# Moving the attention sum and its moments into the recurrence, and joining three stages of a transformer-like layer into one

## The chip, the cores and the metric

The kernel runs on one core of a Trainium2 chip. The core has a matrix engine (PE in the profile, with its weight loads as PEld), a vector engine (DVE), a scalar engine (ACT), a general engine (POOL) and a synchronising engine (SP) that only issues DMAs here. The metric is the device time of one launch in microseconds; lower is better. A profile comes from one execution, and its times are counted from the start of its span.

## The reference, cut to what matters

The input x has 4 sequences (B) of 1,024 rows (T) of 256 numbers (D). Four sublayers follow one another, each adding to x:

```
x = x + recurrence(layernorm(x), ctx)       # scan over 1024 steps
x = x + ffn(layernorm(x))                   # int8 weights, int16 activations
x = x + cross_attention(layernorm(x), ctx)  # 16 heads, 64 context rows
x = x + mixture_of_experts(layernorm(x))    # 8 experts, switch routing

def step(carry, x_t):                       # inside recurrence
    h0, c0, h1, c1, a = carry
    xin = concatenate([x_t, a])
    h0, c0 = lstm_cell(xin, h0, c0, ...)
    h1, c1 = lstm_cell(h0, h1, c1, ...)
    q = h1 @ Wq.T
    attn = softmax(einsum('bh,bsh->bs', q, context))
    a2 = tanh(concatenate([einsum('bs,bsh->bh', attn, context), h1]) @ Wo.T + bo)
    return (h0, c0, h1, c1, a2), a2

def quantize_a16(x):                        # before each of the ffn's two products
    amax = clip(max(abs(x)), 1e-8)          # over the whole tensor
    scale = 32767.0 / amax
    return clip(round(x * scale)) / scale
```

What the recurrence returns at step t is one row of 256 numbers for each of the 4 sequences, and it is needed by step t + 1. The maximum in `quantize_a16` is over the whole tensor, so the ffn's first product can't start before every row is normalised, and its second not before every hidden value is known.

## The kernel before

x lies in the core's own memory as `xres`: 8 groups (NB) of 128 rows for each of the 4 sequences, so 32 tiles of 128 x 256 (NT = 32). The program is a row of stages with a barrier between them, each stage giving every engine its own straight list of instructions and loops. Order is set by that list and by semaphores: an engine waits until a count is reached, and no planner reorders anything.

`front` loads and prepares. `scan` runs the 1,024 steps. PE, ACT and DVE each hold a loop of two steps a turn; on DVE the first 28 steps are written out one by one, since 25 of them carry a piece of other work in the *gaps*: `step(t, s, between)` calls `between(0)` after the first layer's new state, `between(1)` after the second layer's, and `between(2)` after the turned attention sum. In these gaps the ffn's weights are searched for their maximum (128 x 256 at a time, line 431), scaled and rounded. The result of a step is written to `a_hist[:, t, k, b]` by line 496: 128 partitions hold the feature, steps run along the free axis, the eight (k, b) pairs lie interleaved. POOL does nothing in this stage, and SP only loads.

`add_attention_and_normalize` (called the add stage below) then brings a_hist into xres. For each of 32 tiles POOL copies two strided 128 x 128 pieces out of a_hist (line 538), PE turns them, DVE adds them (line 585), takes the row's moments (lines 78 and 81), gets the standard deviation from ACT, normalises (line 89) and searches the tile's largest value (line 599).

`ffn_hidden` makes the 1,024 hidden values of all rows. `ffn_output` multiplies them: DVE quantises a 128 x 1,024 tile in two passes (lines 759 and 762), PE multiplies it in 8 matmuls (line 742; the hardware profile counts each in two records, since they are float32), POOL adds the output's bias to x beforehand, and DVE adds the product (line 768, `finish`). `release_semaphores` clears every semaphore used so far, one instruction each on SP, while all other engines wait at the barrier. `prepare_attention` loads the cross-attention's weights and masks (lines 822 to 827), makes keys and values of the 64 context rows, and `queries` normalises each tile of x, turns it (line 912) and multiplies it (line 922) into the queries of four tiles at a time. Here `in_steps` staggers parts of the work over tiles: `in_steps(eng, [(a, 0), (b, 1)], ...)` runs a on tile t and then b on tile t - 1. Then `attention`, routing and the experts follow, and nothing is changed in their work.

## Time and profile before

| | us |
|---|---|
| three runs | 8344.06, 8344.10, 8343.58 (median 8344.06) |
| the profiled execution | 8346.82 |
| its span in the trace | 8345.0 |

| stage | from | to | length |
|---|---|---|---|
| front | 0 | 54.1 | 54 |
| scan | 54.1 | 7279.9 | 7226 |
| add_attention_and_normalize | 7280.5 | 7353.0 | 72.6 |
| ffn_hidden | 7353.0 | 7451.3 | 98.2 |
| ffn_output | 7451.3 | 7567.9 | 116.6 |
| release_semaphores | 7567.9 | 7574.4 | 6.5 |
| prepare_attention | 7574.4 | 7601.0 | 26.6 |
| queries | 7601.0 | 7676.8 | 75.8 |
| attention | 7676.8 | 7873 | 196 |
| routing, scattering, experts | 7873 | 8345 | 472 |

The stages were read off the timeline: each begins where its first instruction starts. In the rows further down, "busy" is the time in which an engine had an instruction running, `x` is the number of records, and the bracket at the end of a timeline row says how long the engine stood idle just before it and which instruction ended that. PEclk is the share of full speed that the throttle granted PE: 0.50 is 1.2 GHz, 1.00 is 2.4 GHz.

### The profile page before, as it was taken

What the parts mean: (1) busy time and instruction counts of PE and PEld (TensorE: products, weight loads), DVE (VectorE), ACT (ScalarE), POOL (GpSimd) and SP (SyncE); (2) the same over time, 40 slices, a digit from 0 to 9 for tenths busy, and PEclk for the clock granted to TensorE, in tenths of its full rate; (3) what the DMA queues carried; (4) which work ended last, traced back from release to release, by engine and by line L of the source; (5) the groups of instructions that cost most, each with busy time, mean ns of one, the idle gap of its engine ahead of it and who ended that gap; (6) DMA issues with size and microseconds to landing.
All of it is one profiled execution on the core that took longest, in us unless ns stands there. A gap on an engine that the chain in (4) does not pass through costs nothing. (4 is left out here: it accounts for less than half of the span.)

```text
span 8345.0 us, 815594 instructions
## 1 busy us (share of the span) xinstructions
PE 6831.2 (82%) x380504; PEld 5806.1 (70%) x380505; DVE 4214.3 (51%) x21197; ACT 3382.3 (41%) x17078; POOL 332.6 (4%) x342
## 2 busy tenths in 40 slices
PE   7888888888888888888888888888888888766769
PEld 5777777777777777777777777777777777644546
DVE  5555454455454454554544544454454544575822
ACT  4444444444444444444444444444444444432422
POOL 0000000000000000000000000000000000021622
PEclk8999999999999999999999999999999999988879
DMA  2000000000000000000000000000000000000143
GB/s 86 5 0 0 0 0 0 0 0 0 0 0 0 0 0 0 0 0 0 0 0 0 0 0 0 0 0 0 0 0 0 0 0 0 0 6 18 65 165 107
DMA packets 58666, 94.52 MB, mean 11 GB/s; under 512 B 14202, under 2 KB 45952, under 8 KB 57472
## 3 DMA queue, kind: packets, MB, share of 16 engines
q1 hardware_dynamic: 53248, 81.38, 3.0%
q0 software_dynamic: 5376, 12.63, 0.4%
q8 instruction: 20, 0.33, 0.0%
q14 instruction: 22, 0.18, 0.0%
HBM read 76.08 MB, written 20.00 MB: 12 GB/s over the span
## 5 line engine op out<-in xcount | busy, mean ns | idle before, releaser
L307 PE MATMUL scan_sums<-rec_wh,scan_hT 128*4 128x64 f32 x131008 | 2394.2, 219 | 2.6 <-issue 2.5
L428 DVE STREAM_TRANSPOSE scan_sums<-scan_sums 128x64 f32<-128x64 f32 x6144 | 1546.6, 266 | 1137.2 <-PE scan_sums L307 1136.7
L307 PEld LDWEIGHTS scan_sums<-rec_wh,scan_hT 128*4 128x4 f32 x131008 | 1991.4, 89 | 3.4 <-issue 3.4
L307 PE MATMUL scan_sums<-rec_wa,scan_aT 128*4 128x64 f32 (+1 forms) x65536 | 1104.7, 219 | 381.8 <-ACT scan_aT L389 381.8
L307 PEld LDWEIGHTS scan_sums<-rec_wa,scan_aT 128*4 128x4 f32 (+1 forms) x65536 | 915.6, 88 | 570.6 <-ACT scan_aT L389 570.6
L307 PE MATMUL scan_sums<-rec_wx,scan_xT 128*4 128x64 f32 (+1 forms) x65536 | 1291.6, 219 | 7.4 <-issue 6.5
L307 PE MATMUL scan_sums<-rec_wi,scan_hT 128*4 128x64 f32 (+1 forms) x65536 | 1103.1, 219 | 142.5 <-issue 2.5
L307 PEld LDWEIGHTS scan_sums<-rec_wi,scan_hT 128*4 128x4 f32 (+1 forms) x65536 | 914.3, 88 | 331.1 <-DVE scan_hT L478 328.5
L307 PEld LDWEIGHTS scan_sums<-rec_wx,scan_xT 128*4 128x4 f32 (+1 forms) x65536 | 1023.7, 89 | 8.1 <-issue 7.1
L373 ACT ACTIVATE scan_tanh_f<-scan_sums 128x8 f32<-128x8 f32 x2048 | 364.0, 178 | 1188.0 <-DVE scan_sums L428 1188.0
L368 ACT ACTIVATE scan_sums<-rec_bias 128x192 f32<-128x192 f32 x2050 | 686.8, 335 | 302.8 <-PE scan_sums L347 5.5
L389 ACT ACTIVATE scan_aT<-scan_a_sum 128x8 f32<-128x8 f32 x1024 | 182.0, 178 | 1517.8 <-DVE scan_a_sum L493 1517.8
L317 PE MATMUL scan_scores<-rec_kp,scan_hT 128*4 128x64 f32 x16384 | 416.6, 219 | 369.3 <-DVE scan_hT L478 369.3
L317 PE MATMUL scan_a_sum<-rec_vp,scan_pT 128*4 128x64 f32 x16384 | 416.9, 219 | 299.3 <-DVE scan_pT L490 299.3
L375 ACT ACTIVATE scan_scanned<-scan_sums 128x16 f32<-128x16 f32 x2048 | 394.7, 193 | 541.8 <-DVE scan_sums L428 541.8
L317 PEld LDWEIGHTS scan_scores<-rec_kp,scan_hT 128*4 128x4 f32 x16384 | 227.7, 85 | 554.6 <-DVE scan_hT L478 554.6
L478 DVE SCALAR_TENSOR_TENSOR scan_hT<-scan_tanh_o,scan_sums 128x8 f32<-128x8 f32 x2048 | 335.2, 164 | 466.5 <-ACT scan_sums L380 466.5
L317 PEld LDWEIGHTS scan_a_sum<-rec_vp,scan_pT 128*4 128x4 f32 x16384 | 228.0, 86 | 484.6 <-DVE scan_pT L490 484.6
L493 DVE STREAM_TRANSPOSE scan_a_sum<-scan_a_sum 128x64 f32<-128x64 f32 x1024 | 272.2, 266 | 547.7 <-PE scan_a_sum L317 547.7
L482 DVE TENSOR_REDUCE scan_neg_max<-scan_scores 128x1 f32<-128x65 f32 x1024 | 231.4, 226 | 536.1 <-PE scan_scores L317 536.1
L384 ACT ACTIVATE scan_exps<-scan_scores,scan_neg_max 128x65 f32<-128x65 f32 x1024 | 324.9, 317 | 432.1 <-DVE scan_neg_max L482 432.1
L476 DVE TENSOR_TENSOR_SCAN scan_sums<-scan_scanned 128x24 f32<-128x24 f32 x2048 | 443.8, 217 | 71.7
(254 smaller groups left out, 6166.6 us busy)
## 6 DMA issues: line engine op xcount, KB each, us to landing
experts_bias<-in_b SPq DMA_DIRECT2D x40, 640.0 KB, 4.4
moe_w<-in_w SPq DMA_DIRECT2D x16, 1024.0 KB, 12.3
slots_x<-route_blank SPq DMA_DIRECT2D x40, 129.0 KB, 2.5
experts_x<-slots_x SPq DMA_DIRECT2D x40, 129.0 KB
w_xres<-in_x_steps SPq DMA_DIRECT2D x8, 512.0 KB, 11.1
w_xres<-in_x SPq DMA_DIRECT2D x4, 1024.0 KB
x_rows<-w_xres SPq DMA_DIRECT2D x4, 1024.0 KB, 11.3
rec_wh<-in_wh SPq DMA_DIRECT2D x2, 1024.0 KB, 14.8
```

The lines of the kernel that those rows point to most:

```text
L307: last = nc.tensor.matmul(sums[layer][BANK[g]][32 * j:32 * j + ROWS[g], 0:64], state[:, k, FIRST[g]:FIRST[g] + ROWS[g]], weight[:, k, j, 6 ...
L317: last = nc.tensor.matmul(bank[32 * j:32 * j + B, 0:64], state[:, k, :], weight[:, k, j, :], start=start and k == 0, stop=stop and k == 1, ...
L368: nc.scalar.activation(layer_sums[l][:, :, 0:64], w["bias"][:, l, :, :], ACT.Copy).then_inc(seeded[l], 1)
L373: nc.scalar.activation(tanh_f[l][:], gates_of[l][F][:, :, 0:B], ACT.Tanh).then_inc(f_tanh[l], 1)
L375: nc.scalar.activation(ig_terms[l], gates_of[l][IG][:, :, 0:2 * B].rearrange("p k (f b) -> p k f b", f=2), ACT.Tanh).then_inc(c_terms[l], 1)
L384: nc.scalar.activation(exps[:], scores[:, 0:S + 1], ACT.Exp, bias=neg_max[:], accum_out=total).then_inc(exps_done, 1)
L389: nc.scalar.activation(state_of(aT), a_sumT.rearrange("p (k u) -> p k u", k=2)[:, :, 0:B], ACT.Tanh).then_inc(a_ready, 1)
L428: nc.vector.transpose(turned[l][g], sums[l][g][:, 0:64]).then_inc(gates_turned[l][g], 1)
L476: nc.vector.tensor_tensor_scan(cell[l], flat[l][:, 0], flat[l][:, 1], 0.0, ALU.mult, ALU.add).then_inc(c_done[l], 1)
L478: nc.vector.scalar_tensor_tensor(state_of(hT[l]), tanh_o[l][:], 1.0, tanh_c[l].rearrange("p (k b) -> p k b", k=2), ALU.add, ALU.mult).then ...
L482: nc.vector.tensor_reduce(neg_max[:], scores[:, 0:S + 1], AX.X, ALU.max, negate=True).then_inc(max_done, 1)
L493: nc.vector.transpose(a_sumT, a_sum[:, 0:64]).then_inc(a_turned, 1)
```

## The change

It has three parts.

First, in `scan`: when the 128 steps of a group are over, POOL copies their eight (b, k) pieces out of `a_hist` into `part`. In the first four steps of the next group DVE turns them in gaps 0 and 1, one piece a gap (`turn_part`), with its own transposes, which act within blocks of 32 x 32. SP writes them to `a_rows` in DRAM with 32 DMAs so that rows come out in order, and reads the four tiles back into `mid` with one DMA. In steps 7 and 8 of the group DVE adds them to xres (`fold`), in 9 and 10 it takes the row statistics (`spread`), in 11 and 12 it aggregates them, and in 13 it keeps the moments. This is done for groups 1 to 7, so for 28 of the 32 tiles; the last four tiles have no later steps. DVE's loop of steps therefore becomes eight loops, with 14 steps written out ahead of seven of them. PE's and ACT's lists in the scan stay.

Second, `add_attention_and_normalize` adds only the four last tiles, from PE's transposes of a_hist itself. ACT takes one square root for 28 tiles and one for 4, and does the normalising, which DVE did; DVE makes the factors and searches the 32 maxima.

Third, `ffn_output`, `prepare_attention` and `queries` become one stage, `output_and_queries`. In one staggered loop a tile is quantised, multiplied, finished, normalised, turned and projected; keys and values are made at its end. The loads are issued at the start of the stage, and PE and DVE wait for all nine of them (`ALL_LOADS`) before their first tile; the eight loads of masks are issued once the last tile is quantised. Buffers are cut out of `hidden` and `ffn_xn` (class `Arena`). The clearing of semaphores, 128 of them where it was 102, comes after this stage.

The diff, cut to its core:

```diff
+            @block.gpsimd
+            def _(pool):
+                nc.gpsimd.sem_inc(staged, 2 * B)
+                with pool.Fori(1, NB) as g:
+                    for b in range(B):
+                        for k in range(2):
+                            pool.wait_ge(a_kept, g * P)
+                            pool.wait_ge(staged, 2 * B * g)
+                            nc.gpsimd.tensor_copy(part[:, b, k, :], a_hist[:, bass.ds(g * P - P, P), k, b]).then_inc(part_done, 1)
...
+                for g in range(1, NB):
+                    sp.wait_ge(staged, 2 * B * g + 2 * B)
+                    for b in range(B):
+                        rows = a_rows[b, bass.ds(g * P - P, P), :].rearrange("(q r) (j k u) -> j r k q u", q=4, j=4, k=2)
+                        for j in range(4):
+                            for k in range(2):
+                                sp.dma_start(rows[j][:, k], stage[32 * j:32 * j + 32, b, k, :].rearrange("p (q u) -> p q u", q=4)).then_inc(rows_out, 16)
+                    sp.wait_ge(rows_out, ROWS_OUT * g + ROWS_OUT)
+                    sp.wait_ge(folded, B * g)
+                    sp.dma_start(mid[:], a_rows[:, bass.ds(g * P - P, P), :].rearrange("b p d -> p b d")).then_inc(mid_in, 16)
...
+                def turn_part(g, b, k):
+                    dve.wait_ge(part_done, 2 * B * g)
+                    dve.wait_ge(rows_out, ROWS_OUT * g)
+                    nc.vector.transpose(stage[:, b, k, :], part[:, b, k, :]).then_inc(staged, 1)
+
+                def fold(g, b):
+                    x = tile_of(xres, g - 1, b)
+                    dve.wait_ge(mid_in, 16 * g)
+                    nc.vector.tensor_tensor(x, mid[:, b, :], x, ALU.add).then_inc(folded, 1)
...
+                def late(g, at):
+                    def between(gap):
+                        if gap == 2:
+                            return
+                        if at < 4:
+                            turn_part(g, at, gap)
+                        elif 7 <= at < 9:
+                            fold(g, 2 * (at - 7) + gap)
+                        elif 9 <= at < 11:
+                            spread(g, 2 * (at - 9) + gap)
+                        elif 11 <= at < 13:
+                            gather_moments(g, 2 * (at - 11) + gap)
+                        elif at == 13 and gap == 0:
+                            keep_moments(g)
+                    return between
 
...
-                with dve.Fori((PLAIN + 3 * FC + 1) // U, T // U) as i:
+                with dve.Fori((PLAIN + 3 * FC + 1) // U, P // U) as i:
                     t = i * U
                     for s in range(U):
                         step(t, s)
+                dve.wait_ge(ffn["x_in"], 16 * (B + 1))
+                LATE = 14
+                for g in range(1, NB):
+                    for at in range(LATE):
+                        step(g * P + at, 0, late(g, at))
+                    with dve.Fori((g * P + LATE) // U, (g + 1) * P // U) as i:
+                        t = i * U
+                        for s in range(U):
+                            step(t, s)
                 dve.wait_ge(a_kept, T)
+                dve.wait_ge(moments_kept, NB - 1)
...
-                nc.tensor.sem_inc(sum_done, 2)
+                for b in range(B):
+                    for k in range(2):
+                        last = nc.tensor.transpose(turned[b][:, P * k:P * k + P], a_hist[:, P * LAST:P * NB, k, b], w["ident"][:])
+                    last.then_inc(turned_done, 1)
...
+                def normalize(n):
+                    g, b = n // B, n % B
+                    nc.scalar.activation(xn[:, g, b, :], xres[:, g, b, :], ACT.Identity, bias=shift[:, g, b:b + 1],
+                                         scale=rstd[:, g, b:b + 1]).then_inc(xn_done, 1)
+                act.wait_ge(eps_done, 1)
+                deviations(0)
+                for f in range(2):
+                    keep_weight(f)
+                act.wait_ge(shift_done, 1)
+                for n in range(B * LAST):
+                    normalize(n)
+                    if n == 2 * B:
+                        act.wait_ge(moments_done, B)
+                        deviations(1)
+                    if n % B == B - 1 and 2 + n // B < FC:
+                        keep_weight(2 + n // B)
+                act.wait_ge(shift_done, 2)
+                for n in range(B * LAST, NT):
+                    normalize(n)
...
-                in_steps(dve, [(add, 0), (moments, 0), (normalize, 1), (largest, 2)])
+                add(0)
+                factors(0)
+                for b in range(1, B):
+                    add(b)
+                for b in range(B):
+                    spread(b)
+                for b in range(B):
+                    gather_moments(b)
+                for n in range(2 * B + 1):
+                    largest(n)
+                factors(1)
+                for n in range(2 * B + 1, NT):
+                    largest(n)
...
-                in_steps(pe, [(turn, 0), (project, 1)], NB // 2, 2 * B)
...
+                in_steps(pe, [(produce, 1), (turn, 5), (project, 6)], NB // 2, 2 * B)
...
-                in_steps(act, [(deviation, 0), (keep, 1), (keep_queries, 3)], NB // 2, 2 * B)
...
+                in_steps(act, [(deviation, 2), (keep, 5), (keep_queries, 7)], NB // 2, 2 * B)
...
-                in_steps(dve, [(moments, 0), (normalize, 1)])
...
+                dve.wait_ge(loaded, ALL_LOADS)
+                nc.vector.tensor_scalar(h["bq"][:], h["bq"][:], DH ** -0.5, None, ALU.mult).then_inc(built, 1)
+                in_steps(dve, [(finish, 2), (quantize, 0), (moments, 2), (normalize, 3)], NB // 2, 2 * B)
...
+        ALL_LOADS = 16 * (len(loads) + 2)
...
                 for b in range(B):
-                    sp.dma_start(mask_int[:, :, b, :], ins["mask"][b].rearrange("(g p) s -> p g s", p=P)).then_inc(loaded, 16)
-                    sp.dma_start(w["group_prob"][:, :, b, :], ins["fside"][b].rearrange("(g p) s -> p g s", p=P)).then_inc(loaded, 16)
+                    sp.dma_start(mask_int[:, :, b, :], ins["mask"][b].rearrange("(g p) s -> p g s", p=P)).then_inc(masks_in, 16)
+                    sp.dma_start(h["group_prob"][:, :, b, :], ins["fside"][b].rearrange("(g p) s -> p g s", p=P)).then_inc(masks_in, 16)
```

Two helpers of the merged stage, `produce` on PE and `finish` on DVE, wait as follows:

```diff
+                pe.wait_ge(w["out_in"], 32)
+                pe.wait_ge(loaded, ALL_LOADS)
+
+                def produce(i, t):
+                    n = number(i, t)
+                    pe.wait_ge(hq_done, n)
+                    pe.wait_ge(out_done, n)
+                    for f in range(FC):
+                        last = nc.tensor.matmul(summed[t % 2][:, 0:D], hq[t % 2][:, f, :], w["w_out"][:, f, :], start=f == 0, stop=f == FC - 1)
+                    last.then_inc(sum_done, 1)
 
...
+                def finish(i, t):
+                    n = number(i, t)
+                    x = tile_of(xres, *tile(i, t))
+                    dve.wait_ge(bias_done, n)
+                    dve.wait_ge(sum_done, n)
+                    nc.vector.scalar_tensor_tensor(x, summed[t % 2][:, 0:D], back[:], x, ALU.mult, ALU.add).then_inc(out_done, 1)
+
+                def moments(i, t):
+                    dve.wait_ge(out_done, number(i, t) + 2)
+                    norm_moments(nc, dve, norm, number(i, t), t % 2, tile_of(xres, *tile(i, t)))
+
+                def normalize(i, t):
+                    n = number(i, t)
                     dve.wait_ge(turned_done, n)
-                    norm_apply(nc, dve, norm, n, b % 2, tile_of(xres, g, b), xn[b % 2][:]).then_inc(xn_done, 1)
```

### How the order of instructions moves

In the scan DVE's instructions of a looped step stood like this (the first layer's gates, its state `scan_hT`, then the second layer's gates):

```order
L472 SCALAR_TENSOR_TENSOR scan_scanned<-scan_tanh_f,scan_c 128x8 [waits scan_f_tanh0]
L428 STREAM_TRANSPOSE scan_sums<-scan_sums 128x64 [waits scan_summed_o0]
L475 REGISTER_ALU
L476 SCALAR_TENSOR_TENSOR scan_sums<-scan_scanned 128x24 [waits scan_c_terms0]
L478 SCALAR_TENSOR_TENSOR scan_hT<-scan_tanh_o,scan_sums 128x2x4 [waits scan_h_factors0]
L428 STREAM_TRANSPOSE scan_sums<-scan_sums 128x64 [waits scan_summed_f1]
L428 STREAM_TRANSPOSE scan_sums<-scan_sums 128x64 [waits scan_summed_ig1]
```

In the changed program the first written-out step of a group has a turned piece between the two layers, and one behind the second:

```order
L561 SCALAR_TENSOR_TENSOR scan_scanned<-scan_tanh_f,scan_c 128x8 [waits scan_f_tanh0]
L476 STREAM_TRANSPOSE scan_sums<-scan_sums 128x64 [waits scan_summed_o0]
L565 SCALAR_TENSOR_TENSOR scan_sums<-scan_scanned 128x24 [waits scan_c_terms0]
L567 SCALAR_TENSOR_TENSOR scan_hT<-scan_tanh_o,scan_sums 128x2x4 [waits scan_h_factors0]
L517 STREAM_TRANSPOSE scan_stage<-scan_part 128x128 [waits scan_rows_out,scan_part_done]
L476 STREAM_TRANSPOSE scan_sums<-scan_sums 128x64 [waits scan_summed_f1]
```

The second layer's first transpose now stands behind one that waits for POOL's eight copies (`scan_part_done`).

POOL, which had no instruction in the scan, has this at the head of its new loop there, eight copies a turn:

```order
L318 UNCONDITIONAL_BRANCH
L318 ISA
L322 REGISTER_ALU [waits scan_a_kept]
L323 ISA [waits scan_staged]
L323 COPY scan_part<-a_hist 128x128
L323 ISA [waits scan_staged,scan_a_kept]
```

So the first copy is released by the last write of the group (`scan_a_kept`), the next ones follow one another.

On PE, the loop of `ffn_output` had one tile's eight matmuls after another, and behind its end came a barrier and the wait for all loads of `prepare_attention`:

```order
L742 MATMUL output_summed<-ffn_xn 128x256 [waits output_out_done,output_hq_done]
L742 MATMUL output_summed<-ffn_xn 128x256 x7
L736 REGISTER_ALU
L736 COMPARE_AND_BRANCH
L731 UNCONDITIONAL_BRANCH
L842 UNCONDITIONAL_BRANCH [waits barrier_Pool_Activation_PE_DVE_SP_release]
L847 MATMUL heads_k_sum<-heads_ctxT,heads_wk 128x256 [waits heads_loaded]
L847 MATMUL heads_k_sum<-heads_ctxT,heads_wk 128x256 x3
```

In the merged stage a tile's two transposes and every fourth time the queries' four matmuls stand between them:

```order
L942 MATMUL output_summed<-ffn_xn 128x256 [waits output_out_done,output_hq_done]
L942 MATMUL output_summed<-ffn_xn 128x256 x7
L950 MATMUL output_turned<-w_ident,output_xn 128x128 [waits output_xT_done,output_xn_done]
L950 MATMUL output_turned<-w_ident,output_xn 128x128
L956 REGISTER_ALU
L958 ISA [waits output_xT_done]
L960 MATMUL output_q_sum<-ffn_xn 128x512 [waits output_q_done]
L960 MATMUL output_q_sum<-ffn_xn 128x512
L958 REGISTER_ALU
L960 MATMUL output_q_sum<-ffn_xn 128x512 [waits output_q_done]
L960 MATMUL output_q_sum<-ffn_xn 128x512
L939 REGISTER_ALU
```

The transposes and projections of queries, which had a stage of their own, now share PE's list with the ffn's second product.

## Rows read from the trace of the kernel before

**Rows 1.** Busy by stretch: length, PE, PEld, DVE, ACT, POOL (records), PEclk, DMA, GB/s.
```profile
54.00:7280.00 7226.00, 6019.81 (x376780) 5269.86 (x376780) 3617.38 (x19538) 3026.31 (x16387) 0.00 (x0) 1.00 0.00 1
7280.00:7353.00 73.00, 25.09 (x80) 11.96 (x80) 59.41 (x290) 22.78 (x48) 28.06 (x65) 0.50 0.00 0
...
7451.00:7568.00 117.00, 113.50 (x512) 99.10 (x512) 64.98 (x100) 0.00 (x0) 29.09 (x32) 0.97 0.00 0
...
7601.00:7677.00 76.00, 48.93 (x128) 22.24 (x128) 33.64 (x193) 28.44 (x82) 0.26 (x1) 0.84 0.00 0
```

**Rows 2.** Timeline of DVE in a looped step: start, length, instruction, [idle before, releaser].
```profile
7254.75 0.17 DVE L496 TENSOR_SCALAR a_hist<-scan_aT 128x8 f32 x1 [0.35 <-ACT scan_aT L389]
...
7256.55 0.16 DVE L478 SCALAR_TENSOR_TENSOR scan_hT<-scan_tanh_o,scan_sums 128x8 f32<-128x8 f32 x1 [0.23 <-ACT scan_sums L380]
7257.24 0.27 DVE L428 STREAM_TRANSPOSE scan_sums<-scan_sums 128x64 f32<-128x64 f32 x1 [0.53 <-PE scan_sums L307]
```

**Rows 3.** Timeline of DVE, gap 1 of a written-out step with a maximum in it.
```profile
98.11 0.41 DVE L431 TENSOR_REDUCE scan_amax<-ffn_raw 128x1 f32<-128x256 f32 x1
98.72 0.23 DVE L482 TENSOR_REDUCE scan_neg_max<-scan_scores 128x1 f32<-128x65 f32 x1 [0.20 <-PE scan_scores L317]
```

**Rows 4.** POOL's strided copies of the add stage: minimum/median/maximum ns, first and last start.
```profile
L538 POOL COPY first_part<-a_hist x64: 403/410/571, 7280.8 to 7342.3; 128x128 f32 x64
```

**Rows 5.** DVE's SBUF transposes of the scan: busy us, mean ns | idle before.
```profile
L486 DVE STREAM_TRANSPOSE scan_expsT<-scan_exps 128x64 f32<-128x64 f32 x1024 | 230.8, 225 | 0.0
L488 DVE STREAM_TRANSPOSE scan_invT<-scan_inv 128x32 f32<-128x32 f32 x1024 | 184.3, 180 | 0.0
```

**Rows 6.** SP: first and last of nine load issues, the last's landing, and the clears.
```profile
7574.45 0.34 SPq L822 DMA_DIRECT2D heads_ctxT<-in_ctxT  x1
...
7578.15 0.43 SPq L824 DMA_DIRECT2D heads_bo_heads<-in_bo_k  x1
...
DMA to landing us min/median/max: 4.3/4.3/4.3
...
L40 SPq EVENT_SEMAPHORE_RANGE_CLEAR  x102: 25/30/49, 7567.9 to 7574.2; - x102
```

**Rows 7.** Timelines of DVE and ACT: last maxima of the add stage; two 128x256 passes.
```profile
7351.05 0.74 DVE L599 TENSOR_REDUCE first_row_max<-ffn_xn 128x1 f32<-128x256 f32 x2
...
7676.78 0.72 ACT L1038 ACTIVATE attn_q<-heads_q_all 128x256 f32<-128x256 f32 x2 [0.42 <-ACTq L1032]
```

**Rows 8.** Timeline of PE: 67 records of the product, a tile's transposes, a projection.
```profile
7488.72 14.62 PE L742 MATMUL output_summed<-ffn_xn 128*128 128x256 f32 x67
...
7645.19 0.44 PE L912 MATMUL query_turned<-w_ident,query_xn 128*128 128x128 f32 x2 [0.64 <-DVE query_xn L89]
7645.47 3.61 PE L922 MATMUL query_summed<-query_xT,heads_wq 128*128 128x512 f32 x8
```

**Rows 9.** Timeline of DVE in ffn_output: finish, and the quantising's second pass.
```profile
7494.70 0.48 DVE L768 SCALAR_TENSOR_TENSOR w_xres<-output_summed,output_back,w_xres 128x256 f32 x1 [1.58 <-PE output_summed L742]
...
7495.88 0.69 DVE L762 TENSOR_SCALAR ffn_xn<-ffn_xn 128x1024 f32<-128x1024 f32 x1
```

**Rows 10.** Timeline of DVE in prepare_attention.
```profile
7590.02 0.90 DVE L868 COPY heads_twice<-heads_ctxT 128x256 f32<-128x256 f32 x4 [22.42 <-DMA heads_group_prob<-in_fside]
7590.84 1.22 DVE L870 TENSOR_SCALAR heads_neg<-heads_mask_int 128x2048 f32<-128x2048 int32 x1
...
7592.74 4.91 DVE L876 TENSOR_TENSOR heads_keys<-heads_kT,heads_head_mask 128x512 f32<-128x512 f32 x8 [0.60 <-ACT heads_kT L861]
...
7599.01 1.43 DVE L884 TENSOR_TENSOR heads_values<-heads_v,heads_pair_mask 128x256 f32<-128x256 f32 x4
```

**Rows 11.** DMA: instruction fetches in 54 to 285, none in 7300 to 7352, 7259 to 7280.
```profile
q14 instruction: 5, 0.04, 0.1%
...
DMA packets 0, 0.00 MB, mean 0 GB/s; under 512 B 0, under 2 KB 0, under 8 KB 0
...
q8 instruction: 5, 0.08, 1.6%
```

382 lines of the change are left out of this document (182 added, 200 removed).

## The prediction

> **What bounds the kernel now.** I read the table of stretches first [rows 1]. It shows that 7,226 of 8,345 us are the recurrence, where no engine is full: PE is busy 6,020 us and DVE 3,617. A step depends on the one before, so what counts there is a chain through PE, DVE and ACT, 7,226 / 1,024 = 7.06 us a step, and idle time between its links is free for other work. The reader should then look at the add stage: 73 us, DVE busy 59.4, PE at its lower clock and nearly idle. DVE bounds it. In the ffn's output PE is busy 113.5 of 117 us and bounds it. In the queries nothing is full (PE 48.9, DVE 33.6 of 76), and between the two lie 33 us of clearing and loading in which hardly anything computes.
>
> The timeline of a step comes second [rows 2]: DVE writes a_hist at 7254.75 to 7254.92, has the first layer's state at 7256.71 and is idle until the second layer's sums reach it at 7257.24. That 0.53 us is gap 0.
>
> **Scan: what is added.** A group's first gap 0 holds a transpose that waits for eight POOL copies. The copies can start when a_hist is written; I allow 0.3 us for the semaphore and POOL's registers. A copy of this shape took 0.41 us [rows 4], eight take 3.3, so they end at 7254.92 + 0.3 + 3.3 = 7258.5 in the times of [rows 2]. The transpose of 128 columns is not in the trace: 64 took 0.225 and 32 took 0.180 us [rows 5], 0.045 for each further 32, so I take 0.18 + 3 x 0.045 = 0.315, of which some 0.08 overlaps the next instruction (DVE's neighbours start before the one ahead has ended). The second layer's first transpose, due at 7257.24, then starts at about 7258.8: 1.55 us late, with PE, ACT and the rest of the chain waiting behind it. Seven groups: 7 x 1.55 = 10.9 us. With the shortest copy, 0.403, and no allowance it is 8; with the longest, 0.571, (8 x 0.571 = 4.6) it is 7 x 2.85 = 20.
>
> The other inserts I cost at nothing. A 0.41 us maximum in gap 1 still left 0.20 us idle in front of the next reduction [rows 3], so a gap swallows about 0.6 us. The additions of 128 x 256 and the statistics should take 0.4 to 0.5 us (the same width as the maximum), the other transposes 0.32, the aggregations less. If one of the 12 longer inserts of a group spilled over by 0.1 us, that would be 7 x 12 x 0.1 = 8 us, which I keep in the range.
>
> The data must come back before gap 0 of the group's eighth step. The last transpose is issued in gap 1 of the fourth step, about 4.2 us after that step's start, gap 0 lies at 1.8: 4 x 7.06 + 1.8 - 4.2 = 25.8 us. SP issues one DMA every 0.46 us (nine issues, 7574.45 to 7578.15 [rows 6]), so 32 take 14.8 us; a landing took 4.3, and the load back another 0.5 + 4.3. Together 23.9 us: in time by 2 us. DVE also leaves a loop and enters straight code seven times; its step periods before and after its one loop entry in the trace are alike, and I take nothing. Scan: **+11**, from +8 to +28.
>
> **Add stage: what is removed.** DVE's 59.41 us over 32 tiles are 1.86 a tile [rows 1], two of its passes over 128 x 256 being 0.37 each (0.74 for a pair [rows 7]). What stays for the last four tiles is 4 x (1.86 - 0.74) = 4.5 us. Then come 32 maxima; two stand in 0.74 us with 0.41 for one, so they follow each other every 0.33: 10.6 us. The normalising moves to ACT, where two passes of that width took 0.72 us [rows 7], 0.31 to 0.36 each. ACT starts some 4 us before DVE's maxima and has 32 of these and eight copies of turned weights, 40 x 0.36 = 14.4, so it stays just ahead or costs up to 3 us. Lead 1.3 (PE's first transposes at the low clock), roots and factors 0.7, tail to the next stage 1.2 (7351.79, where the last maximum ended, to 7353.0). Sum: 1.3 + 4.5 + 0.7 + 10.6 + 1.2 = 18.3 us where it was 72.6: **-54**, from -50 to -57.
>
> **The merged stage.** Before, output to the start of attention took 7676.8 - 7451.3 = 225.5 us. Now:
> Start: nine loads, 3.7 us of issues and 4.3 to land [rows 6], then one scaling and the first tile's quantising, 1.4 [rows 9], and hand-overs: PE starts at +9.9. This is new: the load's latency is no longer behind anything, and everything behind the wait on PE and DVE stands still.
> Loop: PE has per tile 16 records of 14.62 / 67 = 0.218 us, 3.49, two transposes that hold it for 7645.47 - 7645.19 = 0.28 us, and every fourth tile a projection of 3.5 [rows 8]. Until the last product that makes 32 x 3.49 + 27 x 0.28 + 6 x 3.5 = 140.3, plus 3 for the clock's start (it is at its lower level while PE idles for the loads; before, the output stage lost 113.5 - 111.7 = 1.8 [rows 1]). DVE has per tile finish and quantising, 7494.70 to 7496.57 = 1.87 us [rows 9], and norm work of 33.64 / 32 = 1.05 [rows 1]: 2.9, less than PE's 3.5 to 4.6. So PE bounds it, and the last product ends at +153.2.
> End: finish, moments, root, normalising, transposes, a copy, the last projection and the key product follow one another: 0.5 + 1.1 + 0.3 + 0.3 + 0.4 + 3.6 + 1.8 and 3.5 of hand-overs = 11.5. Behind them DVE's keys 4.9, masks 1.2, values in two steps of 1.4 [rows 10] = 8.9. So +173.6. The mask loads (11.4 us from 7578.6 to 7590.0, where they released DVE [rows 6, 10]) start before the last product and hide behind this.
> Clearing: 102 clears took 6.3 us, 0.062 each [rows 6]; 128 take 7.9, with the barrier 8.6.
> Sum 182.2 against 225.5: **-43**. If PE stayed at 1.2 GHz in the first tiles longer, or hand-overs cost more, -36; if the tail overlaps better, -47.
>
> **Sum.** +10.9 - 54.3 - 43.3 = -86.7. The span of 8345.0 becomes 8258.3. The profiled run took 8346.82, the median of the runs 2.8 less; 8344.06 - 86.7 = 8257.4, and I take **8258 us**. Its own terms range from about 8246 to 8275.
>
> **Rivals.** (a) *The rows come back late.* The 32 stores scatter 128 bytes at a time, which no transfer of the trace does, so their time may be longer than 4.3 us. Every microsecond over the 2 in hand costs 7 us. With 5 us more: 7 x 3 = +21, 8279; this lies against nothing in the profile but the small margin. (b) *The merged loop is bound by a chain, not by PE.* DVE's list puts finish, quantising and normalising in one order, and PE's transposes wait for DVE in the middle of products. If PE waits once a tile for the norm work of 1.05 us, 32 x 1.1 = +35, 8293. For it speaks that DVE's 2.9 us and PE's 3.8 leave under 1 us; against it that transposes lie five steps behind. (c) *The merging overlaps nothing,* so that the joined stage takes its old 225 us: 8301. The order of rows on PE speaks against it, and only a semaphore's count that lags could do it. (d) *Slower: code is fetched again in each turn of a loop.* DVE's list in the scan grows from about 1,500 to 3,900 instructions. In the straight-line start, five pages of 8 KB were fetched for DVE in 231 us, and PE at the end of the scan needed five of 16 KB in 21 us, so up to 3.6 us for one after another is the price [rows 11]. By the program's listing three of the eight DVE loops lie across a boundary of 128 instructions, 57 turns each, 171 turns. If each turn had to fetch both pages again at 3.6 us a turn, this adds 171 x 3.6 = 616, less 87: 8873 us. It decides the sign from 87 / 171 = 0.5 us a turn. Against it: the DVE loop of the add stage lies across such a boundary as well, and between 7300 and 7352 not one packet of code was moved [rows 11].
> The Trainium skill, page "Runtime: NRT & Kernel Launch", section "Instruction fetch mechanics", says that a taken branch forces a fetch if its target isn't in the present window of two pages. By that rule a loop across one boundary stays inside the window and costs nothing, and the trace agrees, with 0 packets in the add stage's loop.
>
> On the copies, the profile shows them slower beside a busy DVE (0.571 at most against 0.403 [rows 4]). The Trainium skill, page "SBUF — State Buffer", has DVE and GpSimd share a port pair as an exclusive lock, held for a whole instruction. By it a copy would wait for a DVE instruction that reads twice from SBUF, and each of the few such in the 3.3 us would add its 0.2 us once a group, 7 x 0.6 = 4 us on the sum above.
>
> **Chances.** The forecast with its own range 0.74; (a) 0.10; (b) 0.06; (c) 0.02; (d) 0.03; something else, spread between 8275 and 8340, 0.05. To hold 8 in 10 the range takes the forecast's terms and most of (a): **8246 to 8288**. A measurement can tell a difference of about 0.2%, 17 us, from none. All but (d) and a little of the last lie below 8327: faster 0.96, same 0.01, slower 0.03.
>
> **What the changed profile would show.** The steps should have a period of about 7.05 us everywhere but in the first step of seven groups, where it should be near 8.6, with DVE idle on POOL's copy. Steps 7 to 13 of a group with longer periods would show spilled inserts, a wait of DVE on the load into `scan_mid` at step 7 would show (a). The add stage should last 18 us with DVE's maxima in a row. The merged stage should begin with 8 us of waiting for loads; then PE should be over 90% busy at 2.4 GHz, with DVE's `finish` released by PE. PE idle on `xn` or `hq` would show (b). Instruction packets in the loops would show (d). The prediction fails if the scan's period in the loops moves at all: 0.02 us there is 18 us.

## The result and the profile after

The changed kernel took 8255.51 us (median of four runs, 8253.7 to 8255.79); the kernel before took 8344.08 on the same chip. The ratio is 0.9892, with a 95% interval of 0.9881 to 0.9904: 88.6 us less, where 86 had been forecast. The profiled execution took 8255.78 us, its span is 8254.0, against 8345.0 before: 91.0 less.

Where the 91 us came from, stage by stage, each counted from its first instruction to the next stage's:

| stretch | before | after | change | forecast |
|---|---|---|---|---|
| front | 54.1 | 55.1 | +1.0 | 0 |
| scan, first instruction to last | 7225.8 | 7230.9 | +5.1 | +10.9 |
| last step to ffn_hidden | 73.1 | 22.9 | -50.2 | -54.3 |
| ffn_hidden | 98.2 | 99.1 | +0.9 | 0 |
| output to attention | 225.5 | 179.5 | -46.0 | -43.3 |
| attention to the end | 668.2 | 666.4 | -1.8 | 0 |

The table of stretches of the changed kernel shows it (length, PE, PEld, DVE, ACT, POOL with records, PEclk, DMA share, GB/s). It answers [rows 1]:

```profile
55.00:7286.30 7231.30, 6016.91 (x376780) 5266.86 (x376780) 3655.59 (x19741) 3026.63 (x16387) 20.62 (x56) 1.00 0.01 2
7286.30:7309.00 22.70, 6.27 (x24) 3.98 (x24) 17.12 (x55) 19.88 (x43) 0.38 (x1) 0.59 0.00 1
...
7408.00:7418.00 10.00, 0.03 (x1) 0.06 (x1) 2.83 (x9) 0.00 (x0) 1.62 (x2) 0.59 0.54 158
7418.00:7430.00 12.00, 12.00 (x44) 10.12 (x45) 6.75 (x12) 1.58 (x2) 11.61 (x15) 0.78 0.01 1
7430.00:7560.00 130.00, 129.69 (x579) 103.90 (x578) 87.23 (x272) 26.14 (x70) 16.84 (x23) 1.00 0.06 10
7560.00:7579.00 19.00, 12.28 (x44) 7.46 (x42) 10.67 (x26) 4.98 (x11) 0.00 (x0) 0.95 0.25 45
7579.00:7587.50 8.50, 0.00 (x0) 0.00 (x0) 0.00 (x0) 0.00 (x0) 0.00 (x0) 0.50 0.00 1
```

The reader should see three things. In the scan DVE is busy 38 us longer than before, and the scan is only 5 us longer: most of the moved work stands in time that was idle. In the short add stage ACT is busier (19.9 of 22.7) than DVE (17.1), which the prediction didn't have. And in the merged stage PE is busy 129.7 of 130 us at full clock, behind 10 us in which it does nothing and 12 at the lower level or mixed.

The timeline of DVE in the first step of a group shows the one place where the scan pays:

```profile
974.52 0.17 DVE L585 TENSOR_SCALAR a_hist<-scan_aT 128x8 f32 x1 [0.35 <-ACT scan_aT L435]
...
976.44 0.16 DVE L567 SCALAR_TENSOR_TENSOR scan_hT<-scan_tanh_o,scan_sums 128x8 f32<-128x8 f32 x1 [0.23 <-ACT scan_sums L426]
977.97 0.31 DVE L517 STREAM_TRANSPOSE scan_stage<-scan_part 128x128 f32<-128x128 f32 x1 [1.37 <-POOL scan_part L323]
978.21 0.35 DVE L476 STREAM_TRANSPOSE scan_sums<-scan_sums 128x64 f32<-128x64 f32 x2
...
979.33 0.16 DVE L567 SCALAR_TENSOR_TENSOR scan_hT<-scan_tanh_o,scan_sums 128x8 f32<-128x8 f32 x1 [0.23 <-ACT scan_sums L426]
```

And POOL's own timeline there, eight copies in one row:

```profile
974.99 2.95 POOL L323 COPY scan_part<-a_hist 128x128 f32 x8 [972.09 <-DVE a_hist L585]
```

DVE waits 1.37 us for POOL. The copies run from 974.99 to 977.94, so one follows another every 0.36 us, though each is recorded with 0.42. The second layer's first transpose starts 3.69 us after the write of a_hist began, where it was 2.49 in [rows 2]: 1.20 late. But the steps are only 0.76 us longer (7.79 for 7.03 in six groups, 7.82 in the one shown). While DVE waited, PE had finished all of the second layer's sums, so the transposes that before waited for them one by one (0.53 and 0.18 idle) now follow at once: from the first of them to the new state it takes 1.12 us instead of 1.42, and another 0.12 comes back at the step's end.

The trace shows a second thing in this step. While POOL copies, the two instructions with which DVE updates the first layer's cell take longer:

```profile
975.52 0.28 DVE L561 SCALAR_TENSOR_TENSOR scan_scanned<-scan_tanh_f,scan_c 128x8 f32<-128x8 f32 x1
...
975.89 0.32 DVE L565 TENSOR_TENSOR_SCAN scan_sums<-scan_scanned 128x24 f32<-128x24 f32 x1
```

In the first step of the seven groups they have 0.24 to 0.28 and 0.30 to 0.32 us, in all other steps at most 0.17 and 0.22, and the first layer's state is about 0.1 us late. It costs nothing here, since DVE then waits for POOL in any case.

### The profile page after: what moved, and what is told of

Same layout as the page of the kernel before. It is cut to its first block and busy times, and to the rows that moved or that the text cites. A ratio compares the mean times of both kernels' runs of the same rounds, so it can differ in the third digit from the quotient of the medians.

```text
span 8254.0 us, 814880 instructions
## 1 busy us (share of the span) xinstructions
PE 6793.0 (82%) x380441; PEld 5788.2 (70%) x380449; DVE 4208.6 (51%) x21164; ACT 3382.8 (41%) x17073; POOL 313.9 (4%) x334
```

## Experiments

Medians of one table aren't from one chip, so each is given with the kernel before beside it. Between the traces of kernels whose looped steps are the same, the mean period of such a step varied from 7.029 to 7.039 us, which is up to 10 us over the scan; for a few microseconds I therefore go by the length of the stage in question in the traces, and by the medians only for the whole.

### The parts alone

One kernel has the scan and the add stage of before and the merged stage of the change; the other the reverse (both are the two programs' functions put together, nothing else is edited).

> The recurrence and the add stage as before, and only the third part of the change: output, preparation and queries as one stage. If the parts are independent, as the comparison of the two traces has it (merged stage 179.5 us where the three stages and the clearing had 225.5), the median is 8344 - 46 = 8298 us, and the scan's period stays at 7.03 us. Rival: the merged stage owes part of its gain to the shorter scan code or the buffers left by the other parts; then its length is not 179.5 but nearer 190.

> The first two parts of the change alone: additions and moments in the recurrence's gaps, and the short add stage; output, preparation and queries as before. By the traces: scan +5.1, add stage 22.4 instead of 72.6, so 8344 + 5 - 50 = 8299 us. The sum of this gain and that of the merging alone should be 90 within 2 us. Rival: the two parts share a gain (for one, fewer stages); then the sum differs by more.

Merging alone: 8298.65 us against 8341.59, 42.9 less (ratio 0.9947, 0.9931 to 0.9964). In its trace the stage up to attention lasts from 7448.1 to 7627.3, 179.1 us. Scan and add stage alone: 8300.24 against 8341.59, 41.4 less (0.9948, 0.9931 to 0.9965); scan 7228.4, add stage 21.9 us, seven steps with a period of 7.77 to 7.81. The two sum to 84.3, not to the 90 within 2 that I expected, and both together gave 88.6; but the interval of each is some 14 us wide either way, so the medians can't tell. The stages' lengths can: they are the same alone and together, but for the scan's 7228.4 against 7230.9, which is the period of the looped steps (7.030 against 7.033). So there is no sign that the parts share a gain, and the merging needs nothing from the rest.

### The wait for POOL in the first gap

```diff
-                        if at < 4:
-                            turn_part(g, at, gap)
-                        elif 7 <= at < 9:
-                            fold(g, 2 * (at - 7) + gap)
...
+                        n = 2 * at + gap
+                        if 1 <= n < 9:
+                            turn_part(g, (n - 1) // 2, (n - 1) % 2)
+                        elif 15 <= n < 19:
+                            fold(g, n - 15)
```

> The changed kernel with every insert of a group one gap later: the first turned piece stands in gap 1 of the group's first step, so that POOL's eight copies have 4 us and not 1.8 before DVE asks for them. My theory: the only cost of the inserts is the wait for POOL in the first gap 0, 0.76 us a group in the trace. It should vanish: every period 7.03, the scan 7 x 0.76 = 5.3 us shorter, 8250 us. Rival: the wait moves to gap 1 or the extra 128x128 transpose in a gap costs by itself; then periods of 7.3 or more stay in the first step, or a later step pays because the rows come back too late (the return has now 0.7 us in hand where it had 5.6).

8247.34 us against 8341.59: 94.3 less (0.9886, 0.9869 to 0.9902). The medians' intervals overlap with the changed kernel's, so the trace decides. In it no step of a group's start is longer any more; of 1,023 periods only the first two, the last two and the eight at which DVE enters a loop stand out. The same transpose, in gap 1:

```profile
979.23 0.16 DVE L568 SCALAR_TENSOR_TENSOR scan_hT<-scan_tanh_o,scan_sums 128x8 f32<-128x8 f32 x1 [0.23 <-ACT scan_sums L426]
979.31 0.31 DVE L517 STREAM_TRANSPOSE scan_stage<-scan_part 128x128 f32<-128x128 f32 x1
979.92 0.22 DVE L572 TENSOR_REDUCE scan_neg_max<-scan_scores 128x1 f32<-128x65 f32 x1 [0.30 <-PE scan_scores L363]
```

It starts at once, and the reduction behind it comes 0.69 us after the state began, as it always does: the insert itself costs nothing. So the wait for POOL was the whole price of the inserts, 7 x 0.76 = 5.3 us. POOL's copies still lengthen DVE's two instructions in the first step (0.23 to 0.28 and 0.30 to 0.32 us), and with no wait behind them the step's period is 6.99 to 7.04, so that is absorbed too. The eight loop entries cost 0.11 us each, seven more than before: 0.8 us, which I had put at nothing.

### How much a gap holds

Both row statistics of steps 9 and 10 in one gap:

```diff
-                            spread(g, 2 * (at - 9) + gap)
+                            if gap == 0:
+                                spread(g, 2 * (at - 9))
+                                spread(g, 2 * (at - 9) + 1, False)
```

> The changed kernel with both row statistics of steps 9 and 10 of a group in gap 0 of the step, one behind the other, and gap 1 left empty. The prediction held that a gap of 0.53 us swallows about 0.6 us of work. Two statistics keep DVE for 0.42 + 0.35 = 0.77 us and should make these two steps 0.1 to 0.2 us longer each (7.15 to 7.25). Rival: a link behind absorbs it, as 0.4 of the 1.2 us of the wait for POOL were absorbed; then they stay at 7.03.

My number was wrong and the rival right: the periods of these steps stay at 7.03 (one run: 8258.13 against 8346.82). The timeline shows how:

```profile
1040.71 0.42 DVE L528 BATCH_NORM_STATS2 scan_stats<-w_xres 128x6 f32<-128x256 f32 x1
1040.73 0.06 DVE L527 MEMSET scan_held<- 128x1 f32 x1
1041.05 0.41 DVE L528 BATCH_NORM_STATS2 scan_stats<-w_xres 128x6 f32<-128x256 f32 x1
1041.38 0.65 DVE L476 STREAM_TRANSPOSE scan_sums<-scan_sums 128x64 f32<-128x64 f32 x2
```

The first transpose begins 0.67 us after the first statistic, 0.76 after the state began; without an insert it is 0.69 [rows 2]. The 0.07 us vanish, since the second transpose has to wait for its own sums anyway. A gap that looks 0.53 us wide took two instructions recorded with 0.83 us together: neighbours overlap by 0.08, and the first link behind the gap has slack of its own.

### How late the rows come back

The additions, and all that follows them, one step earlier:

```diff
-                        elif 7 <= at < 9:
-                            fold(g, 2 * (at - 7) + gap)
+                        elif 6 <= at < 8:
+                            fold(g, 2 * (at - 6) + gap)
```

> The changed kernel with the additions in steps 6 and 7 of a group and all that follows a step earlier. In the trace of the changed kernel the load back is issued at 1017.10 and lands 3.8 us later, at 1020.9, while gap 0 of step 6 opens at about 1019.5. Theory from the trace: that step waits 1.4 us, and its period is 7.03 + 1.4 less what later links absorb (0.4 to 0.5): about 8.0, for seven groups +7 us. By the sum of the prediction (23.9 us from the last transpose to the landing) it would wait 4.4 us and the period be 11; by a third view, that DVE has other work meanwhile, 7.03.

8266.72 us in one run (before: 8346.86), and seven more long periods: 8.10, 8.30, 8.16, 8.05, 8.20, 8.47 and 7.96, on average 1.15 above 7.03. The wait is on the load:

```profile
1020.26 0.16 DVE L567 SCALAR_TENSOR_TENSOR scan_hT<-scan_tanh_o,scan_sums 128x8 f32<-128x8 f32 x1 [0.23 <-ACT scan_sums L426]
1021.94 0.43 DVE L522 TENSOR_TENSOR w_xres<-scan_mid,w_xres 128x256 f32<-128x256 f32 x1 [1.51 <-DMA scan_mid<-a_rows]
```

This is what the trace of the changed kernel said (load issued at 1017.10, landed 3.8 us later), not the 4.4 us of the prediction's sum. That sum had 14.8 us for 32 issues, which took 15.1, but 4.3 for the last store's landing, which takes 1.5, and 4.8 for the load back, which takes 3.8:

```profile
L341 SPq DMA_DIRECT2D a_rows<-scan_stage x224: 303/432/766, 1000.9 to 6422.6; - x112
...
DMA to landing us min/median/max: 1.4/1.5/2.1
```

(these are the changed kernel's 224 stores). So the rows have 5.6 us in hand and not 2. Rival (a), rows that come late in the kernel as it is, falls: no addition in it waits. One step earlier it is true, at 1.15 us a group.

### The wait for the loads

```diff
                 pe.wait_ge(w["out_in"], 32)
-                pe.wait_ge(loaded, ALL_LOADS)
...
                 def project(i, t):
                     if t % B < B - 1:
                         return
+                    pe.wait_ge(loaded, ALL_LOADS)
...
-                dve.wait_ge(loaded, ALL_LOADS)
-                nc.vector.tensor_scalar(h["bq"][:], h["bq"][:], DH ** -0.5, None, ALU.mult).then_inc(built, 1)
...
+                pool.wait_ge(loaded, ALL_LOADS)
+                nc.gpsimd.tensor_scalar(h["bq"][:], h["bq"][:], DH ** -0.5, None, ALU.mult).then_inc(built, 1)
```

> The changed kernel without the wait for all loads at the head of the merged stage: PE waits for them before its first projection, POOL scales the query bias after its first four additions, DVE waits before it copies the context. Theory: the 9.9 us from the stage's start to PE's first product are the loads' 8.0 and 1.9 of quantising, and only the 8 are due to the wait: PE starts at +2.5, the stage is 7.5 us shorter, 8248 us. Rival: PE's stream is held by something else (POOL's bias additions or the lower clock after the idle stretch), and under half of it is won.

8245.95 us against 8341.59: 95.6 less (0.9886, 0.9869 to 0.9902). The merged stage, without the clearing, lasts 164.0 us instead of 170.9, 6.9 less of the 7.5 expected, and PE starts 2.4 us after the stage does. Changed kernel first, then this one:

```profile
7417.97 9.38 PE L942 MATMUL output_summed<-ffn_xn 128*128 128x256 f32 x30 [12.95 <-DVE ffn_xn L1016]
```

```profile
7405.52 10.72 PE L945 MATMUL output_summed<-ffn_xn 128*128 128x256 f32 x35 [5.46 <-DVE ffn_xn L1020]
...
7410.50 2.77 POOL L915 TENSOR_TENSOR w_xres<-w_xres,ffn_xn 128x256 f32<-128x256 f32 x4 [8.21 <-issue]
```

The wait was worth nearly what its latency said. The last row shows the next thing that is late: POOL's first addition comes 7.4 us into the stage though no semaphore that the profile shows holds it back, and the first `finish` needs it; before, this stood hidden behind the loads. (In the second combined version below, where the additions are made earlier, the first `finish` comes at +8.5 instead of +9.0 to +9.2.)

### What bounds the merged loop

Six of the eight products of a tile:

```diff
-                    for f in range(FC):
-                        last = nc.tensor.matmul(..., start=f == 0, stop=f == FC - 1)
+                    for f in range(6):
+                        last = nc.tensor.matmul(..., start=f == 0, stop=f == 5)
```

> The changed kernel, but PE makes only six of the eight products of a hidden tile in the merged stage (what is left out: a quarter of the ffn's second product). If PE bounds the merged loop, as I argued, each tile is 4 x 0.216 = 0.87 us shorter and the stage 32 x 0.87 = 28 us, since DVE's list of 2.9 us a tile still fits under PE's 3.6. If the chain of DVE, ACT and PE bounds it (rival b of the prediction), it is shorter by less than 5 us. In between, DVE or the chain takes over at the tile time that is then seen.

The stage is 150.5 us instead of 170.9: 20.4 less, not 28 and not under 5. The distance between one `finish` and the next tells why. In the changed kernel it is 3.67 us, 7.11 over a projection, and 2.86 and 5.89 to 6.11 here. From the ninth tile on that makes 0.82 us a tile over a turn of eight. But the first six distances are nearly the same in both kernels (3.44, 3.98, 3.76, 3.77, 3.77, 3.67 and 3.33, 3.89, 3.76, 3.77, 3.77, 3.67): there fewer products bring nothing. In this version PE then has idle time and DVE almost none, at full clock (columns as in [rows 1]):

```profile
7433.40:7437.40 4.00, 3.31 (x17) 2.68 (x16) 3.89 (x10) 0.56 (x2) 3.96 (x5) 1.00 0.01 2
```

And behind them, at 2.86, DVE has become the bound as well:

```profile
7488.80 0.48 DVE L1023 SCALAR_TENSOR_TENSOR w_xres<-output_summed,output_back,w_xres 128x256 f32 x1
7489.19 0.75 DVE L1013 TENSOR_SCALAR ffn_xn<-ffn_hidden,output_scale 128x1024 f32 x1
7489.97 0.69 DVE L1016 TENSOR_SCALAR ffn_xn<-ffn_xn 128x1024 f32<-128x1024 f32 x1
...
7490.59 0.42 DVE L96 BATCH_NORM_STATS2 output_norm_stats<-w_xres 128x6 f32 x1
```

No row there has a bracket of idle time. So in the changed kernel PE bounds about 24 of 32 tiles with DVE 0.8 us behind, which is the prediction's 2.9 against 3.7; rival (b) falls for these. For the first eight the next experiment looks for the cause.

### POOL's additions beside DVE's passes

The 32 additions of the output's bias are moved from the merged stage to POOL's list in `ffn_hidden`:

```diff
             @block.gpsimd
             def _(pool):
+                pool.wait_ge(w["out_in"], 32)
+                with pool.Fori(0, NB) as g:
+                    for b in range(B):
+                        x = tile_of(xres, g, b)
+                        nc.gpsimd.tensor_tensor(x, x, w["b_out"], ALU.add).then_inc(biased, 1)
+                pool.wait_ge(biased, NT)
                 pool.wait_ge(max_done, 1)
```

> The changed kernel with POOL's 32 additions of the output's bias moved from the merged stage into the end of the stage before, where POOL is idle. In the merged stage DVE's second quantising pass took 1.10 us while POOL was adding and 0.69 afterwards. Theory: POOL's additions slow DVE and make DVE, not PE, the bound of the first eight tiles; without them every pass takes 0.69 and the first eight tiles come 0.1 to 0.2 us faster each, the stage 1 to 2 us shorter. If the slow passes have another cause (the loads' writes, the low clock) they stay at 1.10. The stage before may be longer, if its DVE passes suffer instead.

In the merged stage every second pass takes 0.69 us, and the distances of the first tiles become 3.45, 3.45, 3.45, 4.2, 3.67, 3.70, 3.77. Their sum is the 25.7 us of the changed kernel: with POOL beside it DVE needs about what PE needs, 3.7 us a tile, so nothing is won there. The stage is 170.0 us instead of 170.9, 0.9 less, just under what I expected, and all of it lies before the first `finish`. Seven traces with the merged stage unchanged have it at 170.6 to 171.4, so the gain is hardly more than their spread. `ffn_hidden` becomes 101.9 us, though, where the traces with it unchanged have 96.6 to 97.7, and the whole is no faster (8259.15 in one run, before 8346.82; the changed kernel beside it took 8256.96). In `ffn_hidden` a quantising while POOL adds, then in the changed kernel, where it does not:

```profile
7380.25 0.66 DVE L834 TENSOR_SCALAR hidden_xq<-ffn_xn,hidden_scale 128x256 f32 x1
7380.94 0.73 DVE L837 TENSOR_SCALAR hidden_xq<-hidden_xq 128x256 f32<-128x256 f32 x1
7381.60 1.26 DVE L849 TENSOR_REDUCE hidden_row_max<-ffn_hidden  x2
```

```profile
7379.90 0.34 DVE L827 TENSOR_SCALAR hidden_xq<-ffn_xn,hidden_scale 128x256 f32 x1
7380.28 0.29 DVE L830 TENSOR_SCALAR hidden_xq<-hidden_xq 128x256 f32<-128x256 f32 x1
...
7383.28 1.28 DVE L842 TENSOR_REDUCE hidden_row_max<-ffn_hidden  x2
```

The scaling and rounding passes go from 0.34 and 0.29 to 0.66 and 0.73 us, the reductions stay, and the last rounding pass, after POOL's last addition, has 0.29 again. So it is POOL that slows them, wherever it adds, and only a certain kind of instruction. It also explains the first tiles of the last experiment: with six products PE would need 2.8 us, and DVE, slowed, still takes 3.7.

### Who bounds the add stage

Every fourth normalising goes to POOL:

```diff
+                pool.wait_ge(shift_done, 1)
+                for n in on_pool:
...
+                    nc.gpsimd.tensor_scalar(xn[:, g, b, :], xres[:, g, b, :], rstd[:, g, b:b + 1], shift[:, g, b:b + 1],
+                                            ALU.mult, ALU.add).then_inc(pool_done, 1)
```

> The changed kernel with every fourth of the 32 normalisings of the add stage on POOL. Theory: the add stage is 4 us longer than forecast since ACT's normalising takes 0.51 us a tile and not 0.33 to 0.36, so ACT and not DVE's maxima bounds it. With 24 tiles on ACT the stage should lose 8 x 0.5 = 4 us less what DVE then bounds: 22.4 becomes 19 to 19.5, 8252 us. Rival: DVE's maxima are held by their own length or by hand-overs; then it stays at 22. POOL could also fail to keep up, if 0.7 us a tile is really 2.

The stage falls from 21.9 to 18.35 us in the trace, 3.5 less (other traces with the stage unchanged have 21.0 to 22.0, so 2.7 to 3.6); the whole is 8254.6 us against 8346.86 (0.9890, 0.9873 to 0.9906), too small a step for the medians to show. In the changed kernel four normalisings take ACT 2.08 us, and DVE stands idle behind them:

```profile
7296.51 2.08 ACT L666 ACTIVATE ffn_xn<-w_xres,first_shift,first_rstd 128x256 f32<-128x256 f32 x4
...
7297.14 1.89 DVE L714 TENSOR_REDUCE first_row_max<-ffn_xn 128x1 f32<-128x256 f32 x4 [0.34 <-ACT ffn_xn L666]
```

With POOL's share DVE's last 23 maxima stand in one row, since the view joins waits as short as those that are left:

```profile
7288.79 3.78 POOL L644 TENSOR_SCALAR ffn_xn<-w_xres,first_rstd,first_shift 128x256 f32<-128x256 f32 x7 [904.91 <-DVE first_shift L719]
...
7294.57 9.52 DVE L728 TENSOR_REDUCE first_row_max<-ffn_xn 128x1 f32<-128x256 f32 x23
```

POOL takes 0.54 us a tile, ACT 0.49 from start to start (2.08 for four, the last of them 0.605 long). But 9.52 us for 23 maxima is 0.41 each, where they follow one another every 0.33 when nothing holds them. In the middle of the row four maxima take 1.74 us, as long as ACT needs for three normalisings and one weight. So ACT still sets the pace of part of the stage, and the rival, that DVE's own length bounds it, holds only for the rest.

### Versions that combine them

The best version has the inserts one gap later, no wait for the loads, and POOL's share of the normalising.

> Three edits together: inserts one gap later (5.3 us), no wait for the loads at the head of the merged stage (6.9 in its trace), and a quarter of the normalisings on POOL (3 to 4 us, if the run beside this one agrees). If they are independent: 8255.5 - 15.5 = 8240 us, on a chip that shows the kernel before at 8344. If POOL's normalising backfires, 8243 or more.

8238.55 us against 8346.86 on the same chip: 108.3 less (0.9871, 0.9855 to 0.9888). The scan is 7226.6 us, the add stage 17.6, the merged one 163.6 before the clearing, where the changed kernel has 7230.9, 21.9 and 170.9: 4.3 + 4.3 + 7.3 = 15.9. It is the fastest kernel here; against the changed one it gains about 16 us by the stages. The two ratios' intervals overlap, but on its chip all its four runs (8236.88 to 8243.22) lie below the four of the version with POOL's share alone (8252.7 to 8256.73).

> The three edits of the best version so far, with every third instead of every fourth normalising on POOL, and the bias additions in the stage before. The add stage should fall from 18.0 to 16.5 us, the first finish of the merged stage should no longer wait for POOL (0.5 us), and the stage should lose 1 to 3 us: 8236 us on a chip that shows the kernel before at 8344. Rival: DVE's maxima bound the add stage by now and nothing falls there.

8245.22 us against 8346.82 (0.9877, 0.9861 to 0.9894): not better. The add stage is 17.05 us, so every third instead of every fourth tile on POOL brings 0.5; the merged stage is 163.0, but `ffn_hidden` 102.4 instead of 96.8 from the moved additions. The looped steps also had a period of 7.039 us in this trace, 7.033 in the other, some 6 us over the scan; what makes the period differ is open.

> The changed kernel once more beside the best version on the same chip: 8255 us, 17 to 20 above the best version. The difference between these two is what the edits are worth.

8256.96 us against 8346.82 (0.9892, 0.9875 to 0.9908), the ratio of the first measurement to the fourth digit. This kernel is 11.7 us above the second combined version, which ran beside it, less than the 17 to 20 that were expected against the best one. The moved additions cost the second version some 5 us in `ffn_hidden`; the rest is open.

## Why the prediction was right, point by point

**The total** was right: -86.7 us of span forecast, -91.0 measured; 8258 us against 8255.5. Its terms were off by up to 6 us either way, and that the total came within 3 us is in part luck: the scan cost 5.8 us less and the merged stage was 2.7 shorter than forecast, the add stage 4.1 longer, so the errors cancelled in part.

**Scan: +10.9 forecast, +5.1 measured.** The mechanism was the right one, shown by moving the inserts a gap later. The step that was mis-sized is "a copy of this shape took 0.41 us [rows 4], eight take 3.3". 0.41 is the length of one copy; the distance between two is 0.36, so eight take 2.95. The transpose's 0.31 us was right to 4 ns. The second error is "1.55 us late, with PE, ACT and the rest of the chain waiting behind it": 0.44 of the 1.20 us that were really lost came back, since PE's sums, made one after another ahead of a DVE that normally waits for each, were all ready. 7 x 0.76 = 5.3, loop entries 7 x 0.11 = 0.8, and the first and the last steps of the recurrence were 1.0 shorter in this trace.

**Gaps.** That the other inserts cost nothing was right, the limit of 0.6 us too low: 0.75 us of work (1040.71 to 1041.46 above) went in and the period did not move.

**The rows' way back**: 23.9 us forecast, 20.0 measured (first store issued at 1000.90, rows back at 1020.9). The landing of a store was taken from a load of another size in [rows 6], 4.3 for 1.5 us, and so was that of the load back, 4.3 for 3.8.

**Add stage: -54.3 forecast, -50.2 measured.** The failed step is "on ACT ... two passes of that width took 0.72 us [rows 7], 0.31 to 0.36 each ... so it stays just ahead or costs up to 3 us". The activation with a scale and a bias for each row takes 0.605 us and comes every 0.49 us; the row I took the price from is a copy of the same width with neither. (In the same stage a copied weight of 128 x 256, also with neither, took ACT 0.37 to 0.39 us; no run changed the operands alone.) With 32 of them and eight weights ACT needs 18 us, and DVE's maxima follow it. Nor did ACT start "some 4 us before DVE's maxima": it was 1.8 us ahead, since a table load of 1.28 us and the square root came first and DVE was ready earlier, 5.0 us into the stage where the forecast had 6.5.

**Merged stage: -43.3 forecast, -46.0 measured.** PE started at +9.9 as forecast (9.8 to 11.2 in six other traces of the same stage, so the exact agreement is luck), the end after the last product took 20.9 (20.4), clearing and barrier 8.6 (8.6). The last product ended at +150.0 instead of +153.2. A tile's products and transposes take 3.67 us where I had 3.49 + 0.28 = 3.77. The products start every 0.216 us, 3.45 a tile, where 14.62 / 67 counted a modelled end; the transposes hold PE for 0.22 and not 0.28; a projection takes 3.44 and not 3.5. That is 32 x 0.04 + 27 x 0.06 + 6 x 0.06 = 3.3 us. DVE, slowed by POOL over the first eight tiles, was in the forecast at 2.9 us a tile and needed 3.7; this cost nothing, since PE needs about as much.

**Rivals.** (a), (b) and (c) fell as told above. (d), code fetched in each turn, is settled by the DMA view of the changed kernel over a group's loop, 1090 to 1860:

```profile
DMA packets 0, 0.00 MB, mean 0 GB/s; under 512 B 0, under 2 KB 0, under 8 KB 0
```

Over the whole program one queue of instruction fetches had 22 before. The change makes only DVE's list much longer, and now this queue has 43 on the page:

```profile
q14 instruction: 43, 0.35, 0.0%
```

and no step of a loop is longer for it but the entry's 0.11 us.

On the copies beside a busy DVE, I had estimated 0.6 us a group from the exclusive lock of the Trainium skill's page "SBUF — State Buffer". In the scan the copies had 0.408 to 0.425 us, so they were not held. It was DVE that was: its two instructions of the first step had 0.24 to 0.32 us instead of 0.15 to 0.22. By the same page whoever issues second waits, and a DVE instruction with two SBUF inputs contends with a POOL instruction that reads SBUF; the trace agrees in so far as DVE's were longer and POOL's, which had started first, were not.

In `ffn_hidden`, where POOL adds, the page's rule that one of the two blocks the other for a whole instruction agrees with the trace in part: passes of 0.29 us became 0.73 beside additions of 0.72, and reductions over 128 x 512 stayed at 0.69. These passes have only one SBUF input, though, and for such the page names a lock only in DVE's 2-port modes, which `tensor_scalar` can enter and `tensor_reduce` can't on trn2. No trace here shows the mode.

## What to carry to other kernels

A chain of small dependent steps has idle stretches that can hold more work than their width shows (0.75 us in 0.53 here), as long as the inserted work itself waits for nothing; it is the wait for another engine, not the work, that should be placed where it has time to end. When several instructions follow one another on an engine, take the distance between their starts, not the recorded length of one; and when a pass moves to another engine, take its price from an instruction with the same operands (here scale and bias by row), not only of the same size. When stages are merged, a wait at the head for loads that only a later part needs should move to that part: here this won 6.9 of the loads' 8.0 us.

## What the runs showed that I had not expected

- A store of 16 KB out of SBUF in 128-byte pieces landed 1.5 us after its issue (1.4 to 2.1, 224 of them); the 512 KB load of the same rows took 3.8.
- A normalising of 128 x 256 numbers with scale and bias by row took ACT 0.605 us (one every 0.49) and POOL 0.54 a tile.
- DVE's in-place passes over SBUF took 0.73 instead of 0.29 us (128 x 256) and 1.10 instead of 0.69 (128 x 1,024) while POOL added; its reductions over 128 x 512 (0.69) stayed. Beside POOL's copies the two small instructions of the cell update went from 0.15 and 0.22 to as much as 0.28 and 0.32.
- The first addition of POOL after its reduction over partitions came 8.1 to 9.3 us later in twelve traces, the kernel before among them, without a semaphore that held it: 8.21 us idle put down to "issue" above. Whether the reduction is the cause wasn't tried.
- The mean period of the looped steps differs between traces of kernels that share them by up to 0.01 us, which is 10 us in 8,250.
